# LSTM recurrent product in column halves, PSUM banks by gate pairs, identity products near the end, last stores on two queues

## What is computed

```
xW = x @ Wx + b                      # RNN, Wx and Wh 512 x 512
h  = tanh(h @ Wh + xW[t])            # h0 = cond_1024
y  = x + all h
a  = y[t] @ Wx + b + h @ Wh          # LSTM, Wx and Wh 512 x 2048
i, f, o = sigmoid(a[:, 0:512]), sigmoid(a[:, 512:1024]), sigmoid(a[:, 1024:1536])
g  = tanh(a[:, 1536:])
c  = f * c + i * g
h  = o * tanh(c)
out = y + all h
```

## Time and profile before

| | |
|---|---|
| median of three runs | 868.7 us |
| the profiled execution's own time | 865.64 us |
| its span | 863.2 us |
| granted TensorE clock, mean over the span | 0.997 |
| TensorE / VectorE / ScalarE / GpSimd busy | 97 / 79 / 64 / 37 % |

### The profile page before, as it was taken

The page is one execution under the profiler, slowest core; times in us unless marked ns, Lnnn a source line. Parts: engine busy times, 40 slices in busy tenths (PEclk is TensorE's granted clock), DMA queues, the critical chain, the costliest instruction groups (busy, mean ns, idle before and its releaser), DMA issues.

```text
span 863.2 us, 50736 instructions
## 1 busy us (share of the span) xinstructions
PE 838.3 (97%) x22208; PEld 605.5 (70%) x22208; DVE 685.8 (79%) x1890; ACT 549.5 (64%) x1509; POOL 320.9 (37%) x678
## 2 busy tenths in 40 slices
PE   7999999999999999999999999999999999999984
PEld 6656655555677777777777777777777787777752
DVE  5788989888677878788778888888878887877663
ACT  3636345565577677676767777676777676777641
POOL 1211266623243434333343434343343434343411
PEclk9999999999999999999999999999999999999998
DMA  8801001110011111001111100011110000000000
GB/s 325 266 3 27 23 7 28 27 28 25 6 28 28 29 27 29 16 17 28 29 28 29 28 16 22 23 29 28 29 28 25 19 5 16 17 16 16 16 15 14
DMA packets 38685, 30.59 MB, mean 35 GB/s; under 512 B 4268, under 2 KB 37184, under 8 KB 37184
## 3 DMA queue, kind: packets, MB, share of 16 engines
q1 hardware_dynamic: 38304, 27.28, 11.1%
q10 hardware_dynamic: 160, 0.08, 0.0%
HBM read 18.95 MB, written 8.39 MB: 32 GB/s over the span
## 4 chain that ended last, share of the span: by engine, by line
PE 85%; DVE 8%; issue 3%; ACT 3%; DMA 0%; ACTq 0%; POOL 0%; POOLq 0%; DVEq 0%
PE ps_l L1039 35%; PE ps_l L1090 25%; PE ps_r L1160 8%; PE ps_r L1179 8%; PE ps_l L1067 3%; PE ps_l L1056 1%; ACT gates L643 1%; PE ps_r L1143 1%; PE ps_r L1133 1%; DVE pre_l L870 1%; DVE fc L877 1%; PE ps_l L1208 1%; DVE ig L879 1%; DVE c L881 1%; DVE hT_r L937 1%
## 5 line engine op out<-in xcount | busy, mean ns | idle before, releaser
L401 POOL TENSOR_TENSOR xb<-xb,h_l 128x128 f32<-128x128 f32 x128 | 59.7, 467 | 433.1 <-DVE h_lo L905 424.8
L643 ACT ACTIVATE gates<-pre_l 128x256 f32<-128x256 f32 x128 | 53.4, 418 | 140.4 <-DVE pre_l L870 140.2
L1039 PE MATMUL ps_l<-whl_hi,hT_hi 128*32 128x512 f16 x2016 | 132.9, 381 | 6.1 <-DVE hT_hi L896 5.1
L1039 PE MATMUL ps_l<-whl_lo,hT_hi 128*32 128x512 f16 x2016 | 132.5, 380 | 0.0
L1039 PE MATMUL ps_l<-whl_hi,hT_lo 128*32 128x512 f16 x2016 | 132.0, 379 | 0.0
L1090 PE MATMUL ps_l<-wxl_hi,wxl_raw 128*32 128x256 f16 x2400 | 116.9, 273 | 1.7 <-ACT wxl_raw L591 1.2
L1090 PE MATMUL ps_l<-whl_raw,wxl_raw 128*32 128x256 f16 x3600 | 115.6, 273 | 0.0
L1090 PEld LDWEIGHTS ps_l<-whl_raw,wxl_raw 128*32 128x32 f16 x3600 | 95.8, 97 | 11.6
L870 DVE SCALAR_TENSOR_TENSOR pre_l<-ps_l,g_products,bias_l 128x256 f32<-128x256 f32 x140 | 60.8, 475 | 51.6 <-PE ps_l L1039 51.4
L1039 PEld LDWEIGHTS ps_l<-whl_lo,hT_hi 128*32 128x32 f16 x2016 | 55.1, 97 | 55.1 <-issue 1.1
L1039 PEld LDWEIGHTS ps_l<-whl_hi,hT_lo 128*32 128x32 f16 x2016 | 54.9, 97 | 54.5
(11 more groups left out here) (143 smaller groups left out, 1888.1 us busy)
## 6 DMA issues: line engine op xcount, KB each, us to landing
xb<-in_x SPq DMA_DIRECT2D x128, 64.0 KB, 2.2
out<-xb SPq DMA_DIRECT2D x128, 64.0 KB, 1.8
whl_raw<-in_L_cond_Wh SPq DMA_DIRECT2D x4, 1024.0 KB, 12.8
wxl_raw<-in_L_cond_Wx SPq DMA_DIRECT2D x4, 1024.0 KB, 17.0
wxr_raw<-in_L_cond_Wx SPq DMA_DIRECT2D x1, 1024.0 KB, 5.6
whr_raw<-in_L_cond_Wh SPq DMA_DIRECT2D x1, 1024.0 KB, 7.6
h0n<-in_cond ACTq DMA_DIRECT2D x1, 64.0 KB
pre_r<-in_L_cond_b ACTq DMA_DIRECT2D x1, 2.0 KB
```

The source lines that it names most:

```text
L401: nc.gpsimd.tensor_tensor(xb[g % NX][:, t, :], xb[g % NX][:, t, :], h_l[s % 2][:, :], ALU.add).then_inc(out_done, 1)
L643: nc.scalar.activation(gates[:, 0:2 * P], pre_l[:, 0:2 * P], ACT.Sigmoid).then_inc(lstm_act, 1)
L1039: last = nc.tensor.matmul(ps_l[s % 4][quarter(j), :], (hT_hi, hT_lo)[h_part][:, k, :], gate_slice(whl[w_part][k], j), start=False, stop=(h ...
```

## The change

From step 28 on recurrent_halves takes the place of recurrent_l. It issues the columns of i and f and those of o and g as separate matmuls of 256 columns, 96 in all. Order: high state parts of i,f; high parts of o,g; low part of i,f, which signals lstm_if_mm; low part of o,g, which signals lstm_mm. cell waits for the first signal before the first half of pre_l and for the second before the second. gates_psum gives the place of a half: one bank holds i,f of both steps of a pair, the next one o,g of both, so that the two halves of a step lie in two banks.

With that, the pair work changes places. Block 7 now runs before block 6, copy_m7 waits for block 5, block 2 stands before the wait for take_u2, pair_last waits for copy_m7 at its start. On ScalarE take_u2 stands behind cell_tanh, and the four calls bias_second, copy_m1, copy_m7, take_u4 stand behind rnn_tanh.

Nine identity products of 128x128 are issued behind the recurrent product of step 126, into ps_pk. The last step's addition to xb moves from GpSimd to VectorE. The last group is stored in two parts: three time steps when step 126 is added, the last one by four transfers of 32 rows, two from SyncE and two from ScalarE.

```diff
+        LAST_PRODUCTS = 9
...
+        def gates_psum(s, half):
+
+            if s < S2:
+                return ps_l[s % 4][:, half * HALF:(half + 1) * HALF]
+            return ps_l[(s - S2) // 2 % 2 * 2 + half][:, s % 2 * HALF:(s % 2 + 1) * HALF]
...
+        def store_last(eng, j):
+
+            done = stored if j < 2 else stored_by_act
+            eng.dma_start(sliced_dram(out, T - TG)[j][:, TG - 1, :], xb[(NG - 1) % NX][quarter(j), TG - 1, :]).then_inc(done, DMA)
...
-            for g in range(NG):
+            for g in range(NG - 1):
...
-            sp.wait_ge(stored, DMA * J * NG)
+
+            sp.wait_ge(out_done, T - 1)
+            for j, dst in enumerate(sliced_dram(out, T - TG)):
+                sp.dma_start(dst[:, 0:TG - 1, :], xb[(NG - 1) % NX][quarter(j), 0:TG - 1, :]).then_inc(stored, DMA)
+            sp.wait_ge(out_done, T)
+            for j in (0, 1):
+                store_last(sp, j)
+            sp.wait_ge(stored, DMA * (J * (NG + 1) - 2))
+            sp.wait_ge(stored_by_act, 2 * DMA)
...
-                if 0 <= k - LAG:
+                if 0 <= k - LAG < T - 1:
                     add_out(k - LAG)
...
             def zero_first(p):
                 s = pair_step(p)
                 act.wait_ge(const_done, 2)
-                act.wait_ge(lstm_pre, 2 * (s - 3))
-                nc.scalar.activation(ps_l[s % 4][:, 0:HALF], zeros, ACT.Copy).then_inc(a_zeroed, 1)
+                act.wait_ge(lstm_pre, 2 * (s - 2))
+                nc.scalar.activation(gates_psum(s, 0), zeros, ACT.Copy).then_inc(a_zeroed, 1)
...
             def copy_m1(p):
-                bank_a = ps_l[pair_step(p) % 4]
+                s = pair_step(p)
                 act.wait_ge(m1_mm, p + 1)
-                nc.scalar.activation(bank_a[:, HALF:GU], bank_a[:, 0:HALF], ACT.Copy).then_inc(m1_copied, 1)
+                nc.scalar.activation(gates_psum(s, 1), gates_psum(s, 0), ACT.Copy).then_inc(m1_copied, 1)
 
             def copy_m7(p):
-                bank_b = ps_l[(pair_step(p) + 1) % 4]
-                act.wait_ge(m7_mm, p + 1)
-                nc.scalar.activation(bank_b[:, 0:HALF], bank_b[:, HALF:GU], ACT.Copy).then_inc(m7_copied, 1)
+
+                s = pair_step(p)
+                act.wait_ge(m5_mm, p + 1)
+                nc.scalar.activation(gates_psum(s + 1, 0), gates_psum(s + 1, 1), ACT.Copy).then_inc(m7_copied, 1)
...
                     gate_values(k - LAG)
                     if pair_at(k) is not None:
                         zero_first(pair_at(k))
+                    cell_tanh(k - LAG)
                     if pair_at(k - 1) is not None:
                         take_u2(pair_at(k - 1))
-                    cell_tanh(k - LAG)
...
-                if pair_at(k) is not None:
-                    copy_m1(pair_at(k))
-                    bias_second(pair_at(k))
-                if pair_at(k - 1) is not None:
-                    copy_m7(pair_at(k - 1))
-                    take_u4(pair_at(k - 1))
                 if t == 0 and G1 <= n - 1 < G2:
                     y_hi(n - 1)
                 if k < T:
                     rnn_tanh(k)
+                if pair_at(k) is not None:
+                    bias_second(pair_at(k))
+                    copy_m1(pair_at(k))
+                if pair_at(k - 1) is not None:
+                    copy_m7(pair_at(k - 1))
+                    take_u4(pair_at(k - 1))
...
+            act.wait_ge(out_done, T)
+            for j in (2, 3):
+                store_last(act, j)
...
-                dve.wait_ge(lstm_mm, s + 1)
+                if s < S2:
+                    dve.wait_ge(lstm_mm, s + 1)
+                else:
+                    dve.wait_ge(lstm_if_mm, s - S2 + 1)
...
                 for half in (0, 1):
-                    cols = slice(half * HALF, (half + 1) * HALF)
-                    nc.vector.scalar_tensor_tensor(out=pre_l[:, cols], in0=ps_l[s % 4][:, cols],
+                    if half == 1 and s >= S2:
+                        dve.wait_ge(lstm_mm, s + 1)
+                    nc.vector.scalar_tensor_tensor(out=pre_l[:, half * HALF:(half + 1) * HALF], in0=gates_psum(s, half),
                                                    scalar=unscale_l(s),
                                                    in1=added[half], op0=ALU.mult, op1=ALU.add).then_inc(lstm_pre, 1)
...
+                if n == T:
+                    dve.wait_ge(y_done, T)
...
-                elif n < T:
+                elif n == T:
+                    g, t = group(s)
+                    dve.wait_ge(lstm_h, n)
+                    dve.wait_ge(out_done, s)
+                    nc.vector.tensor_tensor(xb[g % NX][:, t, :], xb[g % NX][:, t, :], h_l[s % 2][:, :], ALU.add).then_inc(out_done, 1)
+                else:
...
+            def recurrent_halves(s):
+
+                m = s + 1 - N0
+
+                def parts_of(half, *parts):
+                    for h_part, w_part in parts:
+                        for k in range(J):
+                            for j in range(J):
+                                last = nc.tensor.matmul(gates_psum(s, half)[quarter(j), :], (hT_hi, hT_lo)[h_part][:, k, :],
+                                                        gate_slice(whl[w_part][k], j)[:, 2 * half:2 * half + 2, :], start=False,
+                                                        stop=(h_part == 1 and k == J - 1), skip_group_check=True)
+                    return last
+
+                pe.wait_ge(lstm_hT_hi, m)
+                parts_of(0, (0, 0), (0, 1))
+                parts_of(1, (0, 0), (0, 1))
+                pe.wait_ge(lstm_hT_lo, m)
+                parts_of(0, (1, 0)).then_inc(lstm_if_mm, 1)
+                parts_of(1, (1, 0)).then_inc(lstm_mm, 1)
...
             def pair_second(p):
                 if p == 0:
                     pe.wait_ge(t_split, 8)
+                pe.wait_ge(b_biased, p + 1)
                 pe.wait_ge(m1_copied, p + 1)
+                block_product(p, 7, ALL)
                 block_product(p, 6, ALL, m6_mm)
-                pe.wait_ge(b_biased, p + 1)
-                block_product(p, 7, ALL, m7_mm)
 
             def pair_third(p):
+                block_product(p, 2, ALL[:3])
                 pe.wait_ge(u2_out, p + 1)
-                block_product(p, 2, ALL[:3])
                 block_product(p, 5, ALL, m5_mm)
 
             def pair_last(p):
+                pe.wait_ge(m7_copied, p + 1)
                 pe.wait_ge(u4_out, p + 1)
                 block_product(p, 3, ALL)
                 block_product(p, 2, ALL[3:])
-                pe.wait_ge(m7_copied, p + 1)
                 block_product(p, 4, ALL, pair_mm)
...
-                if 1 <= k - LAG:
+                if 1 <= k - LAG < S2:
                     recurrent_l(k - LAG)
+                elif S2 <= k - LAG:
+                    recurrent_halves(k - LAG)
+                if k == END - 2:
+
+                    pe.wait_ge(scale_step, X_STEPS * len(BATCHES))
+                    for _ in range(LAST_PRODUCTS):
+                        nc.tensor.matmul(ps_pk[:, 0:P], ident[:, :], ident[:, :], start=True, stop=True)
```

More of the change, by code:

```diff
@@ L217, in rnn_lstm_kernel @@
         m6_mm = sem("m6_product")
-        m7_mm = sem("m7_product")
         m1_copied = sem("m1_copied")
@@ L225, in rnn_lstm_kernel @@
         lstm_mm = sem("lstm_product")
+        lstm_if_mm = sem("lstm_product_of_i_and_f")
         lstm_pre = sem("lstm_preactivation")
@@ L237, in rnn_lstm_kernel @@
         stored = sem("out_stored")
+        stored_by_act = sem("out_stored_by_scalar")
         END = T + LAG
@@ L572, in bias_second @@
                 g, _ = group(s)
-                nc.scalar.activation(ps_l[(s + 1) % 4][:, HALF:GU], bias_l[:, HALF:GU], ACT.Copy,
+                nc.scalar.activation(gates_psum(s + 1, 1), bias_l[:, HALF:GU], ACT.Copy,
                                      scale=g_inverses[:, 0, g:g + 1]).then_inc(b_biased, 1)
             def copy_m1(p):
-                bank_a = ps_l[pair_step(p) % 4]
+                s = pair_step(p)
                 act.wait_ge(m1_mm, p + 1)
-                nc.scalar.activation(bank_a[:, HALF:GU], bank_a[:, 0:HALF], ACT.Copy).then_inc(m1_copied, 1)
+                nc.scalar.activation(gates_psum(s, 1), gates_psum(s, 0), ACT.Copy).then_inc(m1_copied, 1)
             def copy_m7(p):
-                bank_b = ps_l[(pair_step(p) + 1) % 4]
-                act.wait_ge(m7_mm, p + 1)
-                nc.scalar.activation(bank_b[:, 0:HALF], bank_b[:, HALF:GU], ACT.Copy).then_inc(m7_copied, 1)
+                s = pair_step(p)
+                act.wait_ge(m5_mm, p + 1)
+                nc.scalar.activation(gates_psum(s + 1, 0), gates_psum(s + 1, 1), ACT.Copy).then_inc(m7_copied, 1)
             def take_u2(p):
@@ L590, in take_u2 @@
                 wait(act, in_21_done, p)
-                nc.scalar.activation(u2, ps_l[s % 4][:, HALF:GU], ACT.Copy, scale=unscale[:, g:g + 1]).then_inc(u2_out, 1)
```

(14 more changed lines are left out.)

## The result

The changed kernel took 898.6 us (median of four runs: 902.12, 900.49, 894.8, 896.72) against 868.5 us for the kernel before (four runs), a ratio of 1.035 with a 95 % interval of 1.030 to 1.040. The prediction was 865.5, range 862.0 to 869.3. The sign was wrong, and the time lies 29 us above the range.

A forecast was written before the change was run, and what follows sets the result against it. TensorE's work was taken to bound the steady stage, the recurrence the tail. Steady +1.8, tail -2.2, clock -1.3, last chain -0.4, addition -0.25, stores -0.8 made -3.2 us, off the 868.7 median 865.5, range 862.0 to 869.3.

The forecast's parts named there:

- What bounds the kernel: Steps 28 to 119: TensorE's own work counts one for one; the tail, steps 120 to 127: the recurrence, 5.82 to 5.83 us a tick.
- Part 1: Recurrent product in halves, 92 steady steps: +0.03 us a step, +2.8 us, less 1.0 for waits that go, net +1.8 us.
- rival B: Steady stage: weight loads and instructions cannot be supplied at 27.3 ns a pair; at 34.5 ns +63 us, 930 us; chance 0.05.
- rule of the issue gap: Recurrent product: a straight line from the skill's spacings gives 98 ns at 256 columns, 3.9 us for 2.59; not adopted.
- The 0.02 us wait for hT_r_lo: Recurrent RNN product in even steady steps: the wait goes because the chain comes earlier, 46 x 0.02 = -1.0 us.
- Part 2: Banks by gate pairs and new order on ScalarE and TensorE: no work added, later copies and take_u2 hidden, cost 0.
- Part 3: Tail from step 120: chain 0.39 us shorter, but steps 122 and 124 wait for u2 and gain 0.12 each; -2.2 us.
- Part 4: Nine identity products behind step 126's recurrent product, 2.0 us: TensorE's clock stays at 2.4 GHz, -1.29 us.
- Part 5: End of the kernel: last addition on VectorE -0.25 us, last group's stores split and on two queues -0.8 us.
- C: Rival, faster by more: halves cost nothing extra, or u2 is early and stores bring the full 1.0; 862.2 us, chance 0.21.

The follow-up runs named there:

- split1: Kernel before with only the low-state part of the recurrent product split into 256-column matmuls from step 28, 196 pairs a tick; 869.0 us, 1.0018 of before.
- split2: Kernel before with only the two high-state parts of the recurrent product split into 256-column matmuls from step 28, 212 pairs a tick; 869.9 us, 1.0029 of before.
- split3: Kernel before with all three recurrent product parts split into 256-column matmuls from step 28, same bank, one signal; 893.7 us, run again on another chip 908.8.
- tail: Changed kernel with halves, new banks and new order only for steps 120 to 127; 863.4 us, 0.9953 of before.
- tail_noident: Same as tail but without the nine identity products; 864.0 us, 0.9952 of before.

## Why the prediction was wrong

**What bounds the kernel: right for the kernel before.** Up to 212 pairs a tick TensorE's own work counted one for one in the steady stage (+1.0 and +1.9 us in split1 and split2). At 228 pairs it was no longer the bound; the arrival of its instructions was.

**Part 1, steady stage: wrong, by 39 us (+1.8 forecast, +41.0 in the trace).** The price of a pair was right where pairs flow: 27.3 ns. The failed step is the sentence behind it, "What is late next? Nothing on the rows: TensorE's stream itself." The rows hold a stream of 132 pairs at the full rate, but between 48 wide matmuls, so that a packet was used up in 4.42 us on the mean. It is a rate in a burst, and I took it for the rate of a stage. The measured mean is 6.682 / 228 = 29.3 ns. The prediction had this as rival B, with 28.1 ns as the point from which it decides, and gave it 0.05. Its argument against B, the loads' busy share of 0.76, speaks of the wrong resource: split2's loads are busy for 90 % of the steady stage without a stop (516 of 572 us), the changed kernel's for 91 % with them. The number that would have told was on the page of the kernel before (part 3) and was not read:

```profile
q8 instruction: 174, 2.85, 1.3%
```

It gives the size of a packet, 16.4 KB. That the product in halves uses a packet up in 3.49 us instead of 4.4 could have been worked out; that 3.7 is the limit could not, only that 4.4 was the densest that any row had shown. The right treatment would have been a bound from both sides for 3.49 us and a chance for B of the size of the forecast's.

The Trainium skill, "Runtime: NRT & Kernel Launch", section "Instruction fetch mechanics", says that the instruction memory is refilled in 16 KiB blocks of 256 instructions and that this is hidden, since instructions are dispatched slower than the blocks arrive. The first half agrees with the stops 127 and 128 matmuls apart and with 16.4 KB a packet; the second does not: at 14 ns an instruction asked for, TensorE stood still at the borders.

The Trainium skill's rule of the issue gap ("TensorE: Matmul & The Clock Gate", section "Back-to-back issue gap"), weighed in the prediction, was no help either way: between the stops the halves still run at 27.3 ns, not at the 98 of the estimate from it. The loss came by another mechanism.

**The 0.02 us wait for hT_r_lo:** gone, as forecast; the recurrent RNN product (L1218) takes 0.66 us in both ticks of the chain above.

**Part 2, order and banks: right, cost 0.** Changed kernel and split3 side by side show at most 1.5 us in the whole stage beside the split, and take_u2 holds nothing up in the steady stage.

**Part 3, tail: right in kind, -1.8 for -2.2.** Odd steps took 5.45 to 5.46 us (864.43 - 858.97 for step 121; 5.44 forecast). Even ones took 870.19 - 864.43 = 5.76 with a wait of 0.66 for u2 (5.71 and about 0.8 forecast). Step 126 took 892.31 - 886.85 = 5.46 us. Step 120 gained 0.2 us, not 0.4; in tail it gained 0.36 (5.86 for 6.22).

**Part 4, identity products: the clock stayed, but what kept it is not shown.** Eighteen records in 2.27 us (2.0 forecast), done 0.45 us before the last product (0.8 forecast), which took 894.74 - 892.31 = 2.43 us to its first pre_l (2.4 forecast, 4.11 in the earlier trace rows); the clock stayed at 1.00:

```profile
891.00:896.00 5.00, 3.67 (x104) 3.14 (x102) 2.90 (x9) 1.04 (x4) 0.46 (x1) 1.00 0.09 22
```

But I gave the whole 1.29 us to them, as if the clock fell each time. In tail_noident's profiled execution it stayed without them, at a gap of 2.75 us, and in split3's even at 3.05 us, the gap behind which it had fallen in the kernel before. So the 1.29 us are the price of one execution, not of each, and the trace of the kernel before is one that paid it.

**Part 5, end: right, -1.2 for -1.05.** The addition starts 0.33 us behind h_l's start and ends at 0.62 (0.57 forecast, 0.82 before). The two issues on ScalarE take 0.87 us, 0.43 each, for 0.5 taken, and the end comes 2.5 us after the first issue, 3.5 before. The three quarters stored early took 2.74 us of SyncE for 1.8 forecast, and stayed hidden.

All of tail and end: -4.7 in the trace for -5.0 forecast, of which the 1.3 for the clock is in part the luck of the two executions profiled. The sums of the rivals have slips that decide nothing: C adds up to -3.5, not -3.3, and the 9.2 us of B leave out the 1.0 that comes back (10.3 gives its 28.1 ns). The parts that were worked out to the hundredth were worth a tenth of the one that was settled in a sentence.

## What to carry to other kernels

Price a split of matmuls in instructions as well as in columns: from the page, the instruction queue's packets and the span give how often a packet is used up, and a stage that would use them faster than any stage of the trace has done is unmeasured ground, however well a short burst runs. Here a demand of 128 pairs in 3.75 us cost nothing beyond the pairs' own price, and one in 3.49 us cost 24 to 41 us. Waits on "issue" at equal distances in instructions, in whatever product they fall, are the sign of it; the cure is to split only where the engine waits for others anyway, as in the last eight steps, which gave 863.4 us.

## What was not expected of the hardware

- TensorE's instructions arrived in packets of 16.4 KB (256 instructions), where it stood for them on the mean one in 3.64 to 3.75 us, and the time then differed between two chips: 893.7 and 908.8 us for the same kernel.
- A wait instruction on TensorE for something long fulfilled cost 89 ns between dense matmuls (9600 of them, 856 us).
- The same gap of 3.05 us in TensorE's work was followed by a granted clock of 0.50 in one execution and of 1.00 in another of the same kernel (split3_again, split3). One trace does not tell what a gap costs.
- ScalarE issued 32-row stores in 0.43 us each, SyncE in 0.40; the 1.16 us of the earlier trace rows did not come again.
